# Routed experts computed only for their own tokens, through expert-sorted blocks in DRAM

## The reference

```python
normed = hidden_states * jax.lax.rsqrt(var + 1e-08) * norm_weight
shared = jnp.maximum(normed @ sw1 + sb1, 0.0) @ sw2 + sb2
probs = jax.nn.sigmoid(flat @ router_w.T)          # 8 experts
scores, idx = jax.lax.top_k(probs, 2)
w = scores / (jnp.sum(scores, axis=-1, keepdims=True) + 1e-06)
h = jnp.maximum(jnp.einsum('td,edh->teh', flat, ew1) + eb1[None, :, :], 0.0)
eo = jnp.einsum('teh,eho->teo', h, ew2) + eb2[None, :, :]
routed = jnp.einsum('teo,te->to', eo, comb)        # comb: w at idx, 0 elsewhere
return shared + routed.reshape(b, s, -1)
```

## Time and profile before

| | us |
|---|---|
| three runs | 2029.21, 2031.33, 2031.58 (median 2031.33) |
| profiled execution, its own time | 2029.73 |
| its span, first to last instruction | 2027.9 |
| PE busy in the span | 1939.9 (96%) |
| DVE, ACT, POOL busy | 1514.2, 1379.1, 1130.2 |
| TensorE clock granted, mean | 0.987 of full |

### The profile page before, as it was taken

One profiled execution on the slowest core, in us unless ns is written; L12 is line 12 of the kernel. 1 busy time (PEld: TensorE's weight loads), 2 busy tenths in 40 slices (PEclk: granted clock), 3 DMA queues, 4 the chain that ended last, 5 costly groups with the idle time before them and its releaser, 6 DMA issues.

```text
span 2027.9 us, 37936 instructions
## 1 busy us (share of the span) xinstructions
PE 1939.9 (96%) x12066; PEld 1667.9 (82%) x12066; DVE 1514.2 (75%) x2595; ACT 1379.1 (68%) x2641; POOL 1130.2 (56%) x1370
## 2 busy tenths in 40 slices
PE   4999999999999999899999899999999999999688
PEld 3888888888888888689998788888888888888566
DVE  5988888888888889753223777777777777777575
ACT  3878787878787878554444677777777777776355
POOL 3655555555555555420000877777777777778521
PEclk9999999999999999999999999999999999999699
DMA  4212111111111111100000000000000000100000
GB/s 114 48 44 48 43 47 43 47 43 47 43 47 43 47 43 45 48 14 1 1 1 1 9 4 12 1 10 0 10 0 10 0 10 0 65 1 1 1 5 17
DMA packets 37767, 51.23 MB, mean 25 GB/s; under 512 B 8489, under 2 KB 17714, under 8 KB 37426
## 3 DMA queue, kind: packets, MB, share of 16 engines
q1 hardware_dynamic: 37682, 50.15, 9.7%
HBM read 15.52 MB, written 1.05 MB: 8 GB/s over the span
## 4 chain that ended last, share of the span: by engine, by line
PE 84%; DVE 6%; issue 4%; ACT 3%; POOL 2%; DMA 0%; SPq 0%; ACTq 0%; DVEq 0%; POOLq 0%
PE ps_t L546 7%; PE ps_o L556 7%; PE ps_t L1018 6%; PE ps_o L557 5%; PE ps_s L579 5%; PE ps_s L578 5%; PE ps_s L1429 5%; PE ps_s L1428 5%; PE ps_s L1430 5%; PE ps_t L1494 3%; PE ps_o L1510 3%; PE ps_o L1512 3%; PE ps_o L1511 3%; PE ps_s L999 2%; PE ps_s L1000 1%
## 5 line engine op out<-in xcount | busy, mean ns | idle before, releaser
L1633 DVE TENSOR_REDUCE a_negmax<-ps_s 128x1 f32<-128x1024 f32 x256 | 312.2, 1220 | 65.7 <-PE ps_s L1430 63.0
L1562 ACT ACTIVATE a_p<-ps_s,a_negmax 128x1024 f32<-128x1024 f32 x256 | 286.5, 1119 | 98.1 <-DVE a_negmax L1633 96.8
L720 DVE TENSOR_REDUCE a_negmax<-ps_s 128x1 f32<-128x1024 f32 x256 | 313.4, 1224 | 53.0 <-PE ps_s L579 37.9
L655 ACT ACTIVATE a_pth<-ps_t 128x512 fp32r<-128x512 f32 x512 | 278.6, 600 | 89.9 <-PE ps_t L546 89.8
L706 DVE TENSOR_TENSOR a_ptl<-ps_t,a_pth 128x512 fp32r<-128x512 f32 x512 | 327.4, 681 | 6.5 <-ACT a_pth L655 5.5
L783 POOL TENSOR_SCALAR a_p<-a_p,a_rsum 128x1024 f32<-128x1024 f32 x256 | 289.3, 1130 | 52.8 <-POOL a_rsum L779 52.8
L1728 POOL TENSOR_TENSOR a_p<-a_p 128x1024 f32<-128x1024 f32 x128 | 307.8, 2405 | 10.7
L779 POOL TENSOR_TENSOR a_rsum<-a_sum,minus_one 128x1 f32<-128x1 f32 x256 | 141.4, 552 | 307.4 <-ACT a_p L685 306.2
L685 ACT ACTIVATE a_p<-ps_s,a_negmax 128x1024 f32<-128x1024 f32 x256 | 288.6, 1127 | 15.3 <-DVE a_negmax L720 15.3
L546 PEld LDWEIGHTS ps_t<-ident_r,a_pr 128*128 128x128 f32 x2048 | 200.3, 140 | 32.2 <-POOL a_p L783 4.0
L556 PE MATMUL ps_o<-a_pth,a_v 128*128 128x512 f32 x512 | 219.9, 430 | 3.9 <-ACT a_o L664 1.1
(11 more groups left out here) (242 smaller groups left out, 4540.1 us busy)
## 6 DMA issues: line engine op xcount, KB each, us to landing
a_q<-a_kh SPq DMA_DIRECT2D x64, 128.0 KB, 2.2
a_q<-a_kl SPq DMA_DIRECT2D x64, 128.0 KB, 2.3
a_kh<-a_kh SPq DMA_DIRECT2D x64, 128.0 KB, 2.2
a_kl<-a_kl SPq DMA_DIRECT2D x64, 128.0 KB, 2.3
a_w_raw<-in_l_w SPq DMA_DIRECT2D x8, 384.0 KB, 3.0
f_raw<-in_ffn_w SPq DMA_DIRECT2D x2, 1408.0 KB, 7.6
f_w_raw<-in_ffn_w SPq DMA_DIRECT2D x9, 256.0 KB, 5.0
f_w<-in_ffn_w SPq DMA_DIRECT2D x9, 256.0 KB, 4.3
```

The lines of the kernel that those rows point to most:

```text
L720: dve.tensor_reduce(a0_negmax[:, s % 4:s % 4 + 1], ps_s[:, s % 2, :, :], AX.XY, ALU.max, negate=True)\
L1633: dve.tensor_reduce(a1_negmax[:, s % 2, m:m + 1], ps_s[:, m, :, :], AX.XY, ALU.max, negate=True)\
```

## The change

The shared expert stays as it was: four chunks, `up(c)` and `down(c)`. The eight routed experts are no longer applied to all tokens. The tokens are treated in two groups of 1024 (`GROUPS`, one per batch). For each group:

1. PE and DVE count, for each token and each of its two experts, which row it takes in a table sorted by expert, each expert padded to blocks of 128 rows (`f0_pe_prefix`, `f0_dve_place`). 2 x 1024 rows and padding fill at most NB = 23 blocks; all 23 are always worked on. `f0_expert` holds the expert of each block.
2. POOL scatters the group's rows into a DRAM buffer with 16 indirect DMAs of 128 rows (eight tiles, two experts). The buffer is cleared beforehand by four DMAs in head 1 of a0 (`f0_clear_rows`).
3. SP loads the buffer back. For each block PE turns it over, multiplies by the block's expert (`block_up`, now with tokens on the partitions, three matmuls of 128x512), DVE copies the result out (`block_pre`), PE turns it (`block_turn`), ACT applies bias and relu (`block_relu`), PE multiplies by `w2` (`block_down`), DVE adds the bias (`block_out`), SP stores the rows in rounds of four blocks. PE, ACT and DVE each read the expert's number into a register (`value_load`, shown as TENSOR_LOAD) and address weights or bias with it.
4. POOL gathers each token's two result rows with 16 indirect DMAs, DVE weighs and adds them (`x1_combine`), and the norms follow (`x1_stats` on DVE, `x1_apply` on POOL).

The 46 blocks run as 48 steps, in which block n is multiplied up, n-1 turned and n-2 multiplied down. The first steps of a1 are spread over steps 25 to 46. The constants for the counting are written by POOL at the program's start, ahead of the first norms (`f0_pool_const`, 51 instructions, nearly all of them memsets of a column or a few). Last chunk: norms at slots 1 to 3 of a1, turned at slot 4.

```diff
+    GROUPS = ((0, 1), (2, 3))
+    NG = len(GROUPS)
+    GT = NT // NG
+    NB = (2 * GT * P + NR * (P - 1)) // P
+    ROUND = 4
+    ROUNDS = [list(range(k, min(k + ROUND, NB))) for k in range(0, NB, ROUND)]
+    BLOCKS = NG * NB
...
+            f0_pool_const(pool)
...
+                        f0_clear_rows(sp)
...
+            dve.wait_ge(S["f0_prefix"], g + 1)
+            dve.tensor_copy(f0_rows[:, :, :], f0_prefix_bank(g)).then_inc(S["f0_prefix_out"], 1)
+            dve.wait_ge(S["f0_prefix_out"], g + 1)
...
+            step(dve.tensor_tensor(both, f0_one[:, :, t, :], rows, ALU.mult))
+            step(dve.tensor_reduce(f0_place[:, :, :], both, AX.X, ALU.add))
+            dve.tensor_copy(f0_pos[:, g, :, :], f0_place[:, :, :]).then_inc(S["f0_pos_ready"], 1)
...
+            dve.tensor_scalar(f0_expert[:, g, :], f0_ended[:, :], float(NR - 1), None, ALU.min)\
+                .then_inc(S["f0_expert_ready"], 1)
...
+            pe.matmul(bank, f0_upper[:, :], f0_taken[:, :, :], start=True, stop=False)
+            for s in range(1, GT + 1):
+                ins = pe.matmul(bank[:, s:GT + 1, :], ones[:, :], f0_taken[:, 0:GT + 1 - s, :], start=False, stop=s == GT)
+            ins.then_inc(S["f0_prefix"], 1)
...
+            def load(g):
+                rows = xs_dram[g].rearrange("(n p) d -> p n d", p=P)
+                sp.wait_ge(S["f0_scattered"][g], 16 * 2 * GT)
+                sp.wait_ge(S["f0_xs_turned"], g * len(ROUNDS))
+                sp.dma_start(f0_xs[:, 0:ROUND, :].bitcast(F32), rows[:, 0:ROUND, :]).then_inc(S["f0_xs_first"], 16)
...
+            def store(g, r):
+                blocks = ROUNDS[r]
+                par = (g * len(ROUNDS) + r) % 2
+                sp.wait_ge(S["f0_ys_ready"], g * NB + blocks[-1] + 1)
+                rows = ys_dram[g].rearrange("(n p) d -> p n d", p=P)[:, blocks[0]:blocks[-1] + 1, :]
+                sp.dma_start(rows, f0_ys[par][:, 0:len(blocks), :]).then_inc(S["f0_ys_stored"][par], 16)
+            load(0)
+            for g in range(NG):
+                for r in range(len(ROUNDS)):
+                    if r == len(ROUNDS) - 2 and g + 1 < NG:
+                        load(g + 1)
+                    store(g, r)
...
+            return eng.value_load(f0_expert[0:1, g, j:j + 1], min_val=0, max_val=NR - 1)
...
+            def block_up(n, e):
+                r, cols = f0_round_of(n), f0_cols(n)
+                pe.wait_ge(S["f0_xs_lo_ready"], r + 1)
+                if n > 1:
+                    pe.wait_ge(S["f0_pre_ready"], n - 1)
+                bank = ps_s[:, 0, n % 2, :]
+                w_hi, w_lo = (w[:, bass.ds(e, 1), :].rearrange("p a n -> p (a n)") for w in (f0_w1_he, f0_w1_le))
+                pe.matmul(bank, f0_xs_hi[r % 2][:, cols], w_hi, start=True, stop=False)
+                pe.matmul(bank, f0_xs_hi[r % 2][:, cols], w_lo, start=False, stop=False)
+                pe.matmul(bank, f0_xs_lo[r % 2][:, cols], w_hi, start=False, stop=True).then_inc(S["f0_b_up"], 1)
+            def block_turn(n):
+                pe.wait_ge(S["f0_pre_ready"], n + 1)
+                if n > 1:
+                    pe.wait_ge(S["f0_b_relued"], n - 1)
+                for ht in range(HT):
...
+                    ins = pe.transpose(ps_s[:, 1, n % 2, cols].bitcast(F32R), f0_prer[n % 2][:, cols], ident_r[:, :])
+                ins.then_inc(S["f0_b_turned"], 1)
+            def block_down(n, e):
+                pe.wait_ge(S["f0_b_relued"], n + 1)
+                if n > 1:
+                    pe.wait_ge(S["f0_ys_ready"], n - 1)
+                for ht in range(HT):
+                    ins = pe.matmul(ps_t[:, n % 2, 0:D], f0_bh[n % 2][:, ht * P:(ht + 1) * P],
+                                    f0_w2e[:, bass.ds(e, 1), ht, :].rearrange("p a d -> p (a d)"),
+                                    start=ht == 0, stop=ht == HT - 1)
+                ins.then_inc(S["f0_b_down"], 1)
...
+            up(0)
+            pe.wait_ge(S["a0_out_added"], 2 * H0)
+            f0_pe_logits(pe, 0)
+            f0_pe_turn(pe, 1)
+            down(0)
+            f0_pe_logits(pe, 1)
+            up(1)
+            down(1, lambda: route(0))
+            f0_pe_turn(pe, 2)
+            up(2)
+            pe.wait_ge(S["f0_prefix_out"], 1)
+            f0_pe_logits(pe, 2)
+            down(2)
+            f0_pe_turn(pe, 3)
+            up(3)
+            f0_pe_logits(pe, 3)
+            down(3)
+            route(1)
+            turn_round(0)
...
+            pe.wait_ge(S["f0_shared"], NC)
+            experts = {}
+            for n in range(STEPS):
+                r = f0_round_at(n + 2)
+                if r is not None:
+                    turn_round(r)
+                if n < BLOCKS:
+                    experts[n] = f0_expert_of(pe, n)
+                    block_up(n, experts[n])
+                if 1 <= n < BLOCKS + 1:
+                    block_turn(n - 1)
+                if n >= 2:
+                    block_down(n - 2, experts[n - 2])
+                a1_pe_prepare(pe, n)
+            a1_pe_turn(pe, 2, ps_m)
...
+            def block_relu(n):
+                e = f0_expert_of(act, n)
+                act.wait_ge(S["f0_b_turned"], n + 1)
+                if n > 1:
+                    act.wait_ge(S["f0_b_down"], n - 1)
+                for ht in range(HT):
+                    cols = slice(ht * P, (ht + 1) * P)
+                    ins = act.activation(f0_bh[n % 2][:, cols], ps_s[:, 1, n % 2, cols], ACT.Relu,
+                                         bias=f0_b1[:, bass.ds(e, 1), ht:ht + 1].rearrange("p a b -> p (a b)"))
+                ins.then_inc(S["f0_b_relued"], 1)
...
+            def block_pre(n):
+                dve.wait_ge(S["f0_b_up"], n + 1)
+                if n > 1:
+                    dve.wait_ge(S["f0_b_turned"], n - 1)
+                dve.tensor_copy(f0_pre[n % 2][:, :], ps_s[:, 0, n % 2, :]).then_inc(S["f0_pre_ready"], 1)
+            def block_out(n):
+                r = f0_round_of(n)
+                e = f0_expert_of(dve, n)
+                dve.wait_ge(S["f0_b_down"], n + 1)
+                if f0_round_at(n) is not None and r > 1:
+                    dve.wait_ge(S["f0_ys_stored"][r % 2], 16 * (r // 2))
+                dve.tensor_tensor(f0_ys[r % 2][:, n % NB % ROUND, :].rearrange("p (a d) -> p a d", a=1),
+                                  ps_t[:, n % 2, 0:D].rearrange("p (a d) -> p a d", a=1), f0_b2[:, bass.ds(e, 1), :],
+                                  ALU.add).then_inc(S["f0_ys_ready"], 1)
...
+            for n in range(STEPS):
+                if n < BLOCKS:
+                    block_pre(n)
+                r = f0_round_at(n + 2)
+                if r is not None:
+                    round_lo(r)
+                if n >= 2:
+                    block_out(n - 2)
+                a1_dve_prepare(dve, n)
+            x1_combine(dve, 2)
+            x1_stats(dve, 2, 0)
+            x1_stats(dve, 2, 1)
+            turn_dve(dve, TURN_F0 + 2, 2, ps_m[:, :])
...
+            def scatter(g, i):
+                c = g * GT // TPC + i // TPC
+                if i == 0:
+                    pool.wait_ge(S["f0_pos_ready"], g + 1)
+                    pool.wait_ge(S["f0_zeroed"], 16 * 2 * NG)
+                    pool.wait_ge(S["xst_ready"], NC + (g + 1) * GT // TPC)
+                for k in range(2):
+                    pool.indirect_dma_start(xs_dram[g][:, :], bass.IndirectOffsetOnAxis(ap=f0_pos[:, g, k, i:i + 1], axis=0),
+                                            f0_staged[c][:, i % TPC, :], None).then_inc(S["f0_scattered"][g], 16)
+            def gather(g, i):
+                c = g * GT // TPC + i // TPC
+                if i == 0:
+                    for par in range(2):
+                        pool.wait_ge(S["f0_ys_stored"][par], 16 * (g + 1) * len(ROUNDS) // 2)
+                if i % TPC == 0 and c > 1:
+                    pool.wait_ge(S["f0_combined"], c - 1)
+                for k in range(2):
+                    pool.indirect_dma_start(f0_got[c % 2][:, i % TPC, k, :], None, ys_dram[g][:, :],
+                                            bass.IndirectOffsetOnAxis(ap=f0_pos[:, g, k, i:i + 1], axis=0))\
+                        .then_inc(S["f0_gathered"][c % 2], 16)
...
+            for i in range(GT):
+                scatter(0, i)
+                if i == 2:
+                    norm_rstd(pool, norm_a0(3, 0), 3)
+                if i == 5:
+                    norm_rstd_rms(pool, norm_a0(3, 1), 3)
             a1_wo_scale(pool, 0)
-            for c in range(NC - 1):
-                norm_rstd(pool, c * 2 + NORM_F0, 0)
-                norm_rstd(pool, c * 2 + (NORM_F0 + 1), 1)
+            a1_split_wv(pool, 0)
+            for i in range(GT):
+                scatter(1, i)
+            for i in range(GT):
+                gather(0, i)
+            for c in range(2):
+                for i in range(2):
+                    x1_apply(pool, c, i)
                 a1_keys(pool, c)
```

(43 more changed lines are left out.)

630 lines of the change are left out of this document (352 added, 278 removed).

## The result

| | us |
|---|---|
| changed kernel, four runs | 2054.78 to 2055.70, median 2055.51 |
| before, four runs beside it | 2029.21 to 2032.27, median 2031.45 |
| ratio | 1.0119, 95% interval 1.0103 to 1.0135 |
| profiled execution, and its span | 2054.78, 2053.0 |

A forecast was written before the change was run, and what follows sets the result against it. PE was taken to bound f0 before the change. An a1 start 21 us earlier, less 3, 1 and 1.5 us of costs, gave -16 in total and a forecast of 2014 us, range 1980 to 2062 (the forecast's own 1998 to 2026).

The forecast's parts named there:

- 46 x 2.6 = 120: Block loop in f0: 46 blocks at 2.6 us a step, 120 us, before drain, a1's work and lateness.
- exposed loads at 2060: Rival for the block loop: each step waits 1.7 us for its register load, step 3.7 us, total 2060; chance 0.17.
- POOL as the bound at 2062: Rival: each indirect DMA holds POOL 2.4 us instead of 1.2, 48 us more, total 2062; chance 0.18.
- a step over 3.1: Sign of being wrong, in the block loop: a step longer than 3.1 us instead of the forecast 2.6.
- What goes, what comes: PE work in f0: 204 us of routed positions go, 92 us of blocks come, 112 us won if PE stayed the bound.
- Positions ready at 880.6: Start of f0: norms, routing, prefix and placing done at 880.6 us, when POOL begins to scatter.
- x = 1.2: Scatters and gathers: one indirect DMA of 128 rows holds POOL for 1.2 us, twice SP's issue.
- First block at 919: Start of f0: first block's matmul at 904.8 + 12x = 919 us, x being POOL's time per indirect DMA.
- A step of 2.6: Block loop: PE's 2.0 us of work plus 0.6 us of exposed register load per step.
- Late by 5 us in all: Group 1's steps: norms of chunks 0 and 1 on POOL come about 5 us later than DVE and PE want them.
- Last block at 1052, gap 34.9, a1 at 1087: End of f0: last block at 1052, PE idle for 34.9 us, a1 starting at 1087 against 1108 before, -21 us.
- Chunk 3 in a1's first slots, +3: Start of a1: chunk 3's norms a slot later, with 2.8 us of combining ahead, cost 3 us.

The follow-up runs named there:

- The record: First series of the unedited changed kernel, with late semaphore updates of PE: median 2055.5 us, ratio 1.0119; its profiled execution took 2054.78.
- after_again: The changed kernel run again, nothing edited, in another series and without late updates: 2023.0 us, ratio 0.9963.
- pe_fixed: Changed kernel with a fixed expert per block on PE, so no register loads and fixed addresses there: 2020.1 us; repeated in a series with late updates, 2048.2.
- w1_late: Changed kernel with POOL's last five w1 splits (L976) moved behind chunk 3's second norm: 2019.3 us, ratio 0.9943.
- late_turns_tail: Changed kernel with chunks 0 and 1 turned and a1's first queries made behind the last block, chunk 2's second norm ahead of the last four gathers: 2011.8 us.
- after_fifth: The changed kernel, nothing edited, in a further series, with late updates: 2053.0 us, ratio 1.0110.
- after_sixth: The changed kernel, nothing edited, in a further series, with late updates: 2054.0 us, ratio 1.0116.
- the paced version: Changed kernel with a1 started behind the last block, plus pauses between the indirect DMAs of scatter 1 and gather 0: 2007.7 us, ratio 0.9879.

## Why the prediction was wrong

The step that failed is the block loop: "46 x 2.6 = 120", drain 3, a1's work 5 and lateness 5, 133 us in all. The record has 150. The terms themselves were generous (119 in after_again); what was missing is a term for the end of PE's instructions being told to other engines up to 17.7 us late beside dense indirect DMAs, 31 us. None of my rivals had it: the one that ended near the time, exposed loads at 2060, is wrong in its mechanism, since the load costs 0.06 us of a step and not 1.7; so is POOL as the bound at 2062, which needs x = 2.4. One of my signs of being wrong, a step over 3.1, can be read as met in the record, where the mean is 3.3; but six long steps make it, and the usual one took 2.2. Without late updates the kernel is 0.4% faster than before, so the sign I gave holds in three series of six; even there it wins 8 us, not the 17 of the forecast.

Point by point, with after_again, which has no such stall:

- *What goes, what comes*: right. PE's busy time fell by 89 us, where 112 were counted at full clock. 5 to 7 of the difference are PE's work in a step, 2.10 (pe_fixed) to 2.16 and not 2.0; the rest I put down to matmuls at half clock around the gaps (granted 0.75 from 852 to the first block), which is an estimate.
- *Positions ready at 880.6*: 888. The step assumed chunk 2's apply at chunk 1's price, 1.1 us; it took 4.94 beside POOL's five L976. And the prefix, 1.7 us in my sum, ran at half clock: its 16 records took 3.5. Chunk 2's first apply took 2.06 instead of 1.1. I quoted the row that shows this lock and applied it to scatters only. w1_late, without it, had positions at 883.2.
- *x = 1.2*: right: 0.94 to 0.96 busy and 0.30 between, 1.25 to 1.26, for 56 of the 64 (after_again). The other eight hold POOL for 1.05 to 1.39, most of them the first behind other work of POOL; two of the eight, 1.14 and 1.29, lie beside or just behind DVE's apply at 897.77, which itself took 1.32.
- *First block at 919*: 930. 7.5 us are the positions. Two more are POOL's twelve DMAs with the norms between them (20.4 us from positions to chunk 3's apply, where 18.4 were in the sum), and the last 1.6 are in PE's steps behind them: the granted clock was 0.67 to 0.76 from 870 to 930, and I had put every product there at full clock.
- *A step of 2.6*: 2.16 for steps 8 to 20. Of the 0.6 for the load, 0.06 came.
- *Late by 5 us in all* for the norms in group 1's steps: steps 36 to 45 took 3.6 us each instead of 2.3, 11 us more. late_turns_tail takes 8 of it out.
- *Last block at 1052, gap 34.9, a1 at 1087*: 1049.4, 36.3 and 1085.7. Errors of opposite sign cancelled up to here; PE was idle for 35.6 us of the gap. The chain of the gap in after_again, start and length, is the predicted list of landing, combining, statistics, apply and gather:

```profile
1061.80 2.51 DMA f_got<-f_ys_rows,f_pos
...
1064.34 1.15 DVE Y L1682 x4
...
1066.91 0.88 DVE stats L348 x4
...
1069.23 1.05 POOL rstd L368
...
1073.71 1.26 POOL X L1710
...
1075.14 1.08 POOL f_got L1427
...
1081.73 3.14 POOL Y L1705 x4
...
1084.92 1.11 PE ps_m L442 x4
```

- *Chunk 3 in a1's first slots, +3*: +11.7 (a1's first score to the 129th matmul took 208.2 us against 196.5). This is the second term that was mis-sized. It counted the combining at its own 2.8 us. The waits of PE behind a1's start, in after_again, are:

```profile
PE ps_m L442 <- POOL Y L1705: 35.6, 1, 35.6
PE ps_t L442 <- issue: 9.0, 1, 9.0
PE ps_s L1732 <- ACT a_p L1868: 3.9, 4, 1.7
PE ps_t L1503 <- DVE a_q L1538: 3.8, 1, 3.8
```

In before the longest is 5.0 us in three pieces. DVE's combining stands ahead of the next query's low part and of the next maximum and, beside POOL's work on the slot, takes 4.7 us instead of 2.4; the turning at slot 4 then waits 9.0 us for POOL's second apply.

Summed: -22.3 at a1's start, +11.7 in its first slots, +1.6 behind them: -9.0 of span where I had -16; and +34 in a series with late updates. The range, 1980 to 2062, held all of them, the first by way of a mechanism that was not in it.

The Trainium skill (SBUF — State Buffer, Who interferes with whom) speaks of a lock between DVE's and POOL's ports; the 4.94 us apply agrees, and w1_late's 1.11 and 4.96 show it following the splits. It does not account for the late updates: the late ones were all PE's, while POOL's indirect DMAs themselves kept their 1.26 us.

## What to carry to other kernels

Run the unedited kernel in every series: four unrelated edits looked like a remedy here. A wait that the profile puts down to no engine is worth a comparison of the instruction's end with its semaphore's update. When work is taken off the bound engine and a wait for a chain on slower ones is put in, ask first what other work can be moved into the gap: that (with late turns) was worth 27 us here, the change itself 8.

## What the runs showed of the hardware

- Semaphore updates of PE came up to 18.3 us late (after_fifth and after_sixth) while POOL issued indirect DMAs 1.26 us apart and PE worked beside them, in four of nine series (chips 7, 4, 13 and the record's; not on 15, 3, 6 and 0; on 5 only the paced version ran). Of the updates of other engines that the traces hold none did; 19 to 34 of all engines are missing from each such trace. In the same series scatter 0, beside other work of PE, had none. At 2.35 us apart there were none in the one run that tried it. Why some series and not others is open (each had a chip and an occasion of its own, and nothing separates the two), and so is why PE.
- An indirect DMA of 128 rows of 512 bytes holds POOL for 0.94 to 0.96 us, with 0.30 to the next, whichever its direction (up to 1.4 us where other work of POOL stood ahead), and lands 2.2 (scatter) or 2.5 us (gather) after its issue.
- A register load from SBUF usually takes 0.28 us on ACT and 0.30 on PE and DVE, and one in a step of 2.1 us is hidden but for 0.06.
